# Four layers of cross attention on one core: equal value units and a new order in the third and first steps

## The chip, the cores and the metric

The program runs on one core of a Trainium2 chip. The metric is the time of one execution in device microseconds (us). All data is 32-bit floating point. The profiled execution took 2264.95 us, of which 2263.2 us lie between its first and its last instruction.

## What is computed

64 batches of 128 positions with 160 channels go through four attention layers, one after the other; each layer reads the same context of 77 tokens with 256 channels. 20 heads of 8 channels. Cut to what matters:

```python
q = heads(x @ Wq); k = heads(ctx @ Wk); v = heads(ctx @ Wv)
out = softmax(q @ k.T / sqrt(8)) @ v                   # layers 0 to 2
x = x + merge(out) @ Wo + bo
# layer 3: text = ctx[:, :73], image = ctx[:, 73:]
p = softmax(q @ k_text.T / sqrt(8)); text_out = p @ v_text
sem = normalize(p @ text) @ normalize(image).T         # image scores, per head
fused = q @ k_ip.T / sqrt(8) + 0.5 * sem
ip_out = (softmax(fused) * mask) @ v_ip
x = x + merge(text_out + ip_out) @ Wo + bo
```

The layers in the code are numbered 0 to 3. The norm of `p @ text` is computed through the Gram matrix of the text tokens: `p G p` summed over tokens.

## The kernel before

**Steps.** Each engine runs the same sequence of steps `t`. Step `t` starts item `c = t`: layer `c % 4` of batch `c // 4 - c % 4`. So four steps bring in one new batch, and four batches are under way, each in another layer. The steps are called here by `t % 4`: step 0 starts layer 0 of a batch, step 3 layer 3. An item takes several steps: its scores in step `c`, its second scores (scores transposed, for the exponentials) in step `c + 1`, its product with the values in `c + 2`, its output in `c + 3` (layer 3: `c + 7`, since its image branch comes first). Twenty-four steps are the body of a loop that runs 9 times; the steps before and after it are unrolled.

**The order inside a step** is written by hand for every engine (`step` of each block). TensorE: `scores(t)`, `turn_out`, `queries(t+1)`, `values` (step 3), `product(t-2)`, `project_out`, `image` (the Gram matrix, step 3), `turn_top(t)`, `second(t-1)`, `turn_back(t-2)`. In steps 1 and 2 it also has the four waves of the Gram product, two in each (`gram_wave`); in every even step the keys of one layer for two batches (`keys`: in step 0 at the end, in step 2 ahead of the second scores). One step in 24 has `image_tokens` too.

**PSUM.** `ps_s` (four banks) holds scores, and then the second scores of the item before; `BANKS = (3, 0, 1, 2)` is the order in which they are read. `ps_c` (two buffers) holds products and outputs. `ps_k` is one bank, shared by all units: keys, image tokens, values, Gram matrix and Gram waves. A unit waits until the one before it has been read (`units_done`).

**ScalarE** writes the exponentials (`exps`, from `ps_s` to `p_t`), in layer 3 first in place (`text_exps`), and copies queries, products, outputs, keys and values out of PSUM. **VectorE** reduces the maxima of the scores (`top_of`), subtracts them in layer 3 (`less_top`), multiplies the Gram waves by the probabilities (`weigh`), normalizes the product (`results`, which `turn_out` of the next step waits for through `o_ready`), adds the residual (`new_x`), and computes the image branch in 20 small steps (`image_branch`), each of which waits for the one before. **GpSimd** spreads the keys into blocks (`k_blocks`, two instructions an item), and folds the weighted Gram rows. **SyncE** issues the DMAs, among them the four of each item that carry the maxima to `q_sb` (`move_top`), which the second scores wait for.

**Values.** `values` computes 448 columns (4 layers x 112: two heads of every group of three) and `values_rest` the other 224, after the first have been read; ScalarE copies the first with two instructions of 224 elements and the second with one.

## Time and profile before

| | |
|---|---|
| median of 3 runs | 2264.23 us (2263.96 to 2268.26) |
| the profiled execution | 2264.95 us, span 2263.2 us |
| TensorE matmul busy | 2086.4 us (92%), 26394 matmuls |
| VectorE busy | 1481.7 us (65%) |
| ScalarE busy | 1075.1 us (48%) |
| GpSimd busy | 458.7 us (20%) |
| mean granted TensorE clock | 0.970 |

Lines of the trace give the start in us from the span's start, the time taken, engine, source line, operation, `output<-input` with shapes, and the number of instructions merged in the line. In brackets stands the idle time of that engine ahead of it and what ended it. PE is TensorE's matmul, PEld its weight load, DVE VectorE, ACT ScalarE, POOL GpSimd. An f32 matmul appears as two instructions. The ends of matmuls are modelled, so that a busy TensorE may in truth be waiting; starts are better evidence.

### The profile page before, as it was taken

The page shows a single profiled execution, that of the slowest core. Times are in us where ns is not written, and L with a number is a line of the kernel's source. Part 1 is how long each engine was busy: PE and PEld are TensorE (multiplying, and loading weights), DVE is VectorE, ACT ScalarE, POOL GpSimd, SP SyncE. Part 2 cuts the span into 40 slices and gives each one's busy share as a digit, 9 for nine tenths or more (in the row PEclk, how much of TensorE's full clock was granted, in tenths as well). Part 3 has the DMA queues.
Part 4 walks back from the last instruction along what each step waited for, and adds up shares of the span by engine and source line. Part 5 has one row for each costly group of instructions (what it writes and reads, how often), then busy time and mean ns, then how long its engine had stood idle before and what let it go on. Part 6 is the DMA issues. An engine that isn't in the chain of part 4 may idle for free.

```text
span 2263.2 us, 75842 instructions
## 1 busy us (share of the span) xinstructions
PE 2086.4 (92%) x26394; PEld 1697.5 (75%) x26394; DVE 1481.7 (65%) x4449; ACT 1075.1 (48%) x2733; POOL 458.7 (20%) x870
## 2 busy tenths in 40 slices
PE   2699999999999999999999999999999999999975
PEld 1567877887787788778778877887887788778764
DVE  3236776777677676767767766776676677667654
ACT  0245554455445455544545554554554455555431
POOL 0112122212212221221222122122212222222110
PEclk9889999999999999999999999999999999999975
DMA  3111111211111121112111111211211121111000
GB/s 82 49 43 50 52 43 42 52 50 39 47 52 44 41 52 51 38 46 52 45 41 52 52 38 47 53 44 40 52 52 38 47 53 44 39 53 38 22 10 5
DMA packets 108576, 101.31 MB, mean 45 GB/s; under 512 B 42240, under 2 KB 84952, under 8 KB 108184
## 3 DMA queue, kind: packets, MB, share of 16 engines
q1 hardware_dynamic: 104556, 92.88, 15.1%
q8 instruction: 231, 3.78, 0.7%
q10 hardware_dynamic: 3628, 3.33, 0.6%
q14 instruction: 161, 1.32, 0.2%
HBM read 34.13 MB, written 5.41 MB: 17 GB/s over the span
## 4 chain that ended last, share of the span: by engine, by line
PE 78%; SPq 8%; DVE 5%; issue 4%; DMA 2%; ACT 2%; ACTq 1%; DVEq 0%; POOLq 0%; POOL 0%
PE ps_s L738 11%; PE ps_c L816 10%; PE ps_s L771 8%; PE ps_c L886 6%; PE ps_k L839 6%; PE ps_k L644 5%; PE ps_q L717 5%; PE ps_c L875 4%; PE ps_k L670 4%; PE ps_s L788 4%; PE ps_k L844 4%; SPq L584 3%; PE ps_c L891 3%; PE ps_c L852 2%; SPq L577 2%
## 5 line engine op out<-in xcount | busy, mean ns | idle before, releaser
L1131 DVE TENSOR_REDUCE top<-ps_s 128x6 f32<-128x462 f32 (+3 forms) x1024 | 511.3, 546 | 88.2 <-PE ps_s L738 84.3
L1027 ACT ACTIVATE p_t<-ps_s 116x512 f32<-116x512 f32 (+1 forms) x768 | 372.9, 545 | 48.9 <-PE ps_s L771 46.9
L738 PE MATMUL ps_s<-k_blocks,q_sb 32*128 32x231 f32 (+1 forms) x3584 | 347.8, 384 | 20.3 <-issue 18.5
L816 PE MATMUL ps_c<-p_t,v_rows 116*27 116x128 f32 (+1 forms) x7168 | 288.7, 284 | 14.8 <-DMA v_rows<-v_img 12.3
L738 PEld LDWEIGHTS ps_s<-k_blocks,q_sb 32*128 32x128 f32 x3584 | 229.9, 185 | 84.9 <-issue 31.3
L816 PEld LDWEIGHTS ps_c<-p_t,v_rows 116*27 116x27 f32 (+1 forms) x7168 | 214.1, 108 | 86.5 <-issue 49.3
L1055 ACT ACTIVATE o_t<-ps_c 128x256 f32<-128x256 f32 x256 | 98.1, 383 | 368.3 <-PE ps_c L875 302.7
L1354 POOL TENSOR_TENSOR k_blocks<-k_sb,mask_k 128x231 f32<-128x231 f32 x384 | 211.8, 573 | 267.6 <-PE ps_s L771 252.5
L771 PE MATMUL ps_s<-q_sb,k_blocks 32*116 32x128 f32 (+1 forms) x5376 | 223.8, 283 | 27.7 <-DMA q_sb<-top_t 15.0
L839 PE MATMUL ps_k<-gram,p_t 116*128 116x154 f32 x896 | 210.6, 317 | 41.6 <-DVE weighted L1171 41.6
L771 PEld LDWEIGHTS ps_s<-q_sb,k_blocks 32*116 32x116 f32 (+1 forms) x5376 | 186.3, 175 | 63.7 <-issue 52.0
L1363 POOL TENSOR_TENSOR weighted<-weighted 128x720 f32<-128x720 f32 x64 | 93.0, 1453 | 679.3 <-DVE weighted L1171 679.3
L1171 DVE TENSOR_TENSOR weighted<-ps_k,probs 128x462 f32<-128x462 f32 (+1 forms) x256 | 142.6, 557 | 118.2 <-PE ps_k L844 118.2
L644 PE MATMUL ps_k<-context,wk 128*128 128x154 f32 (+1 forms) x1024 | 159.4, 299 | 40.8 <-DVE minus L1122 40.2
L886 PE MATMUL ps_c<-o_t,wo_lead 128*128 128x128 f32 x1024 | 185.8, 305 | 2.4 <-ACT o_t L1055 2.4
L839 PEld LDWEIGHTS ps_k<-gram,p_t 116*128 116x128 f32 x896 | 137.2, 193 | 66.4 <-DVE weighted L1171 57.9
L886 PEld LDWEIGHTS ps_c<-o_t,wo_lead 128*128 128x128 f32 x1024 | 136.7, 194 | 56.1 <-issue 52.1
L1282 DVE SCALAR_TENSOR_TENSOR x_out<-ps_c,bias,x_work 128x128 f32<-128x128 f32 x64 | 22.5, 351 | 234.9 <-PE ps_c L891 234.9
L644 PEld LDWEIGHTS ps_k<-context,wk 128*128 128x128 f32 x1024 | 142.5, 194 | 42.9 <-issue 42.9
L1040 ACT ACTIVATE u_sb<-ps_c 128x256 f32<-128x256 f32 x256 | 98.1, 383 | 160.9 <-PE ps_c L816 160.9
L844 PE MATMUL ps_k<-gram,p_t 115*128 115x115 f32 (+1 forms) x896 | 166.1, 266 | 0.0
L891 PE MATMUL ps_c<-o_t,wo_tail 32*128 32x128 f32 x1024 | 164.3, 280 | 0.0
(118 smaller groups left out, 3595.3 us busy)
## 6 DMA issues: line engine op xcount, KB each, us to landing
v_rows<-v_img SPq DMA_DIRECT2D x128, 227.4 KB
context<-in_ctx SPq DMA_DIRECT2D x64, 336.0 KB, 3.0
q_sb<-top_t SPq DMA_DIRECT2D x576, 6.0 KB
v_rows<-v_img SPq DMA_DIRECT2D x64, 115.2 KB
v_rows<-v_img SPq DMA_DIRECT2D x64, 112.2 KB
v_rep<-v_dram SPq DMA_DIRECT2D x64, 50.0 KB
q_sb<-top_t SPq DMA_DIRECT2D x192, 2.0 KB
gram<-g_img SPq DMA_DIRECT2D x64, 46.3 KB
```

What stands on the lines that cost most here:

```text
L644: ins = pe.matmul(o[:, :, 0:n], w_rows(wk, l, kt, m, 128), cx_pair(p, kt, 0, n), start=kt == 0, stop=kt == 1)
L738: ins = pe.matmul(ps_s[:, z * 512 + j * GT:z * 512 + j * GT + n], q_sb[c % 3][lo:lo + QUAD, j * S:(j + 1) * S], k_blocks[c % 3][lo:lo + QU ...
L771: ins = pe.matmul(ps_s[0:n, to:to + S], k_blocks[c % 3][lo:lo + QUAD, col:col + n], q_sb[c % 3][lo:lo + QUAD, j * S:(j + 1) * S], start=Tr ...
L816: ins = pe.matmul(ps_c[t % 2][32 * (g % 4):32 * (g % 4) + UC, g // 4 * S:(g // 4 + 1) * S], v_rows[b % NC][0:n, v:v + UC], p_t[c % 3][0:n, ...
L839: pe.matmul(ps_k[:, to:to + 2 * T], p_t[c % 3][0:n, at:at + S], gram[b % NX][0:n, 0:2 * T], start=j == 0, stop=False, skip_group_check=True)
L844: ins = pe.matmul(ps_k[:, to:to + m], p_t[c % 3][0:n, at:at + S], gram[b % NX][0:n, 2 * T:2 * T + m], start=False, stop=True, skip_group_c ...
L886: pe.matmul(ps_c[(t - LAG) % 2][:, j * S:(j + 1) * S], o_rows(wo_lead, l, j), o_t[:, 0:S], start=j == 0, stop=False, skip_group_check=True)
L891: ins = pe.matmul(ps_c[(t - LAG) % 2][:, j * S:(j + 1) * S], o_rows(wo_tail, l, j)[TAIL:LEAD, :], o_t[TAIL:LEAD, S:2 * S], start=False, st ...
L1027: act.activation(to, source, ACT.Exp, scale=SCALE).then_inc(p_ready, 1)
L1131: dve.tensor_reduce(top[c % 2][:, z * BH:z * BH + m], s.rearrange("p (h t) -> p h t", t=T)[:, :, 0:n], AX.X, ALU.max).then_inc(s_top, 1)
L1171: dve.tensor_tensor(weighted[:, lo * T:hi * T], ps_k[:, 0:(hi - lo) * T], probs[:, lo * T:hi * T], ALU.mult).then_inc(w_ready, 1)
L1354: pool.tensor_tensor(k_blocks[c % 3][:, j * GT:(j + 1) * GT].rearrange("p (h t) -> p h t", t=T), keys_of(l, b // 2)[:, at:at + T].unsqueez ...
```

## The change

It changes four things. The values are computed in two equal units, layers 0 and 1 and then layers 2 and 3: each has matmuls of 224 and of 112 columns, and three copies of 112 elements on ScalarE. In step 2 one Gram wave now stands ahead of the second scores, one behind them, and the keys are last. On VectorE, steps 8 to 15 of the image branch stand ahead of `results` in step 0, steps 16 to 18 behind it in the same step (before: in step 1), the new x of layer 3 stands behind `results`, and the wave products follow the waves. On ScalarE the image exponential stands ahead of the exponentials, and the last text exponential at the end of step 3. SyncE and GpSimd are untouched.

```diff
             def units_done(k, t):
...
+                if k is None or t % 4 == 2:
+                    pe.wait_ge(k_evac, raised(k, e_keys, t))
             def keys(k, t):
...
                     units_done(k, t - 1)
+                if e_waves(t):
+                    pe.wait_ge(w_ready, raised(k, e_waves, t, per=2))
...
+            def values_unit(b, u):
+                w = wv[:, :].rearrange("p (l k a n) -> p l k a n", l=L, k=2, a=2)[:, 2 * u:2 * u + 2]
+                third = w.rearrange("p l k a (g i d) -> p l k a g i d", g=TRI, i=2)
+                for kt in range(2):
+                    pe.matmul(ps_k[0:T, 0:2 * VN].rearrange("p (l n) -> p l n", l=2), cx(b, kt, 0, T),
+                              w[:, :, 0, kt, :], start=kt == 0, stop=kt == 1)
+                for kt in range(2):
+                    ins = pe.matmul(ps_k[0:T, 2 * VN:VU].rearrange("p (l g d) -> p l g d", l=2, g=TRI),
+                                    cx(b, kt, 0, T), third[:, :, 1, kt, :, 1, :], start=kt == 0, stop=kt == 1)
+                return ins
...  TensorE, step
-                if e_waves(t) and t % 4 == 1:
+                if e_waves(t):
                     gram_wave(k, t, 0)
-                if e_keys(t) and t % 4 == 2:
-                    keys(k, t)
...
                     second(k, t - 1)
                 if e_waves(t) and t % 4 == 2:
-                    gram_wave(k, t, 0)
+                    gram_wave(k, t, 1)
                 if exists(t - 2):
                     turn_back(k, t - 2)
-                if e_waves(t):
+                if e_waves(t) and t % 4 == 1:
                     gram_wave(k, t, 1)
-                if e_keys(t) and t % 4 == 0:
+                if e_keys(t):
                     keys(k, t)
...  ScalarE
+            def values_out(u):
+                for i in range(GH):
+                    to = v_img[i][:, 2 * u * VL:2 * (u + 1) * VL].rearrange("p (g u) -> p g u", u=UC)
+                    if i < 2:
+                        source = ps_k[0:T, 0:2 * VN].rearrange("p (g u) -> p g u", u=2 * D)[:, :, i * D:(i + 1) * D]
+                    else:
+                        source = ps_k[0:T, 2 * VN:VU].rearrange("p (g u) -> p g u", u=D)
+                    ins = act.activation(to[:, :, i * D:(i + 1) * D], source, ACT.Copy)
+                return ins
...  ScalarE, step
                 if ip(t):
-                    for i in range(4):
+                    for i in range(3):
                         text_exps(k, t, i)
-                for i in range(2):
-                    if exists(t - 1):
-                        exps(k, t - 1, i)
                 if ip(t - 6):
                     image_exp(k, t - 6)
-                for i in range(2, 4):
-                    if exists(t - 1):
+                if exists(t - 1):
+                    for i in range(4):
                         exps(k, t - 1, i)
-                if e_keys(t) and t % 4 == 0:
+                if e_keys(t):
                     keys(k, t)
                 if e_values(t):
                     values_rest(k, t)
+                if ip(t):
+                    text_exps(k, t, 3)
...  VectorE, step
-                if e_waves(t) and t % 4 == 1:
+                if e_waves(t):
                     weigh(k, t, 0)
                 if ip(t - 5):
                     norms(k, t - 5)
                     image_branch(k, t - 5, 1, 8)
-                if ip(t - 6):
-                    image_branch(k, t - 6, 16, 19)
-                if out(t):
+                if out(t) and not ip(out_step(t)):
                     new_x(k, t)
-                if e_waves(t) and t % 4 == 2:
-                    weigh(k, t, 0)
+                if ip(t - 5):
+                    image_branch(k, t - 5, 8, 16)
                 if ip(t - 6):
                     image_branch(k, t - 6, 19, 21)
                     image_weights(k, t - 6)
+                if e_waves(t) and t % 4 == 2:
+                    weigh(k, t, 1)
                 if exists(t - 2):
                     results(k, t - 2)
-                if e_waves(t):
+                if out(t) and ip(out_step(t)):
+                    new_x(k, t)
+                if ip(t - 5):
+                    image_branch(k, t - 5, 16, 19)
+                if e_waves(t) and t % 4 == 1:
                     weigh(k, t, 1)
-                if ip(t - 5):
-                    image_branch(k, t - 5, 8, 16)
```

## Rows read from the trace of the kernel before

**Rows 1.** Who waited for whom on TensorE, 600 to 1800 us: total, times, longest

```profile
PE ps_k L839 <- DVE weighted L1171: 21.4, 36, 0.6
PE ps_s L771 <- DMA q_sb<-top_t: 6.0, 9, 1.1
```

**Rows 2.** Timeline, step 3: last subtraction of the maxima, then second scores

```profile
947.00 0.60 DVE L1146 TENSOR_TENSOR probs<-ps_s,top 128x438 f32<-128x438 f32 x1
...
947.75 0.81 PE L771 MATMUL ps_s<-q_sb,k_blocks 32*116 32x128 f32 x19
```

**Rows 3.** Timeline, end of step 3: exponentials, second value unit, scores of layer 0

```profile
948.82 1.83 ACT L1027 ACTIVATE p_t<-ps_s 116x256 f32<-116x256 f32 x4
...
949.11 0.92 PE L681 MATMUL ps_k<-wv,context 128*77 128x224 f32 x4
...
949.96 1.42 PE L738 MATMUL ps_s<-k_blocks,q_sb 32*128 32x231 f32 x12
...
950.52 0.38 ACT L997 ACTIVATE v_img<-ps_k 77x224 f32<-77x224 f32 x1
950.71 0.31 PEld L738 LDWEIGHTS ps_s<-k_blocks,q_sb 32*128 32x128 f32 x8 [0.19 <-ACT p_t L1027]
```

**Rows 4.** Timeline, step 0 and the start of step 1, VectorE and TensorE

```profile
951.50 1.96 DVE L1131 TENSOR_REDUCE top<-ps_s 128x2 f32<-128x154 f32 x4 [0.20 <-PE ps_s L738]
951.68 0.44 PE L875 MATMUL ps_c<-ident,o_sb 128*128 128x128 f32 x2
...
956.13 0.36 DVE L1284 SCALAR_TENSOR_TENSOR x_work<-ps_c,bias,x_work 32x128 f32<-32x128 f32 x1
...
956.54 1.05 PEld L644 LDWEIGHTS ps_k<-context,wk 128*128 128x128 f32 x8
...
956.85 0.30 DVE L1184 RECIPROCAL recip<-ps_c 128x21 f32<-128x21 f32 x1 [0.36 <-PE ps_c L852]
...
957.18 0.33 DVE L1192 TENSOR_TENSOR o_sb<-ps_c,recip 128x168 f32<-128x168 f32 x1
...
957.73 0.67 PE L738 MATMUL ps_s<-k_blocks,q_sb 32*128 32x231 f32 x8
...
958.73 0.44 PE L875 MATMUL ps_c<-ident,o_sb 128*128 128x128 f32 x2
...
959.27 0.24 DVE L1245 TENSOR_TENSOR z_c<-z_b,rs_y 128x80 f32<-128x80 f32 x1
```

**Rows 5.** The same stretch: GpSimd's key blocks beside image steps 8 and 9

```profile
956.95 1.10 POOL L1354 TENSOR_TENSOR k_blocks<-k_sb,mask_k 128x231 f32<-128x231 f32 x2
...
957.43 0.17 DVE L1234 SCALAR_TENSOR_TENSOR rs_t<-rs_x,rs_y 128x24 f32<-128x24 f32 x1
957.63 0.46 DVE L1237 TENSOR_TENSOR rs_u<-rs_t,rs_y 128x24 f32<-128x24 f32 x1
```

**Rows 6.** Timeline, ScalarE's exponentials in steps 1 and 2, and layer 2's scores

```profile
963.03 0.98 ACT L1027 ACTIVATE p_t<-ps_s 116x256 f32<-116x256 f32 x2 [0.33 <-PE ps_s L771]
...
964.07 1.08 ACT L1027 ACTIVATE p_t<-ps_s 116x512 f32<-116x512 f32 x2
...
965.20 0.31 PEld L738 LDWEIGHTS ps_s<-k_blocks,q_sb 32*128 32x128 f32 x8 [0.20 <-ACT p_t L1027]
...
971.26 1.96 ACT L1027 ACTIVATE p_t<-ps_s 116x256 f32<-116x256 f32 x4
```

**Rows 7.** Timeline, TensorE from step 2's second scores to step 3's scores

```profile
970.49 0.81 PE L771 MATMUL ps_s<-q_sb,k_blocks 32*116 32x128 f32 x19
...
971.58 0.53 PE L839 MATMUL ps_k<-gram,p_t 116*128 116x154 f32 x2
...
973.63 0.53 PE L839 MATMUL ps_k<-gram,p_t 116*128 116x154 f32 x2 [0.61 <-DVE weighted L1171]
...
974.24 0.67 PE L738 MATMUL ps_s<-k_blocks,q_sb 32*128 32x231 f32 x8
```

**Rows 8.** Timeline of another batch, step 0: first matmuls of the image tokens

```profile
721.39 1.07 PE L654 MATMUL ps_k<-ip_six,wkip 128*128 128x24 f32 x8
```

More of the change, by code:

```diff
@@ L47 @@
 VL = TRI * UC
+VU = 2 * (VN + TRI * D)
 LEAD = 128
@@ L625, in units_done @@
                     pe.wait_ge(w_ready, raised(k, e_waves, t, per=2))
+                if k is None or t % 4 == 2:
+                    pe.wait_ge(k_evac, raised(k, e_keys, t))
                 if k is None:
                     pe.wait_ge(six_evac, raised(k, e_six, t))
-                    pe.wait_ge(k_evac, raised(k, e_keys, t))
             def keys(k, t):
@@ L661, in image_tokens @@
                 ins.then_inc(six_psum, 1)
+            def values_unit(b, u):
[8 more added lines that the diff above has]
+                return ins
             def values(k, t):
-                b = values_batch(t)
                 units_done(k, t - 1)
-                w = wv[:, :].rearrange("p (l k a n) -> p l k a n", l=L, k=2, a=2)
-                for kt in range(2):
-                    ins = pe.matmul(ps_k[0:T, 0:L * VN].rearrange("p (l n) -> p l n", l=L), cx(b, kt, 0, T),
-                                    w[:, :, 0, kt, :], start=kt == 0, stop=kt == 1)
-                ins.then_inc(v_psum, 1)
+                values_unit(values_batch(t), 0).then_inc(v_psum, 1)
             def values_rest(k, t):
-                b = values_batch(t)
                 pe.wait_ge(va_evac, raised(k, e_values, t))
-                w = wv[:, :].rearrange("p (l k a g i d) -> p l k a g i d", l=L, k=2, a=2, g=TRI, i=2)
-                for kt in range(2):
-                    ins = pe.matmul(ps_k[0:T, 0:L * TRI * D].rearrange("p (l g d) -> p l g d", l=L, g=TRI),
-                                    cx(b, kt, 0, T), w[:, :, 1, kt, :, 1, :], start=kt == 0, stop=kt == 1)
-                ins.then_inc(vb_psum, 1)
+                values_unit(values_batch(t), 1).then_inc(vb_psum, 1)
             def image(k, t):
@@ L691, in image @@
                     units_done(k, t - 1)
-                at = L * TRI * D
+                at = VU
                 for kt in range(2):
@@ L828, in gram_wave @@
                     pe.wait_ge(p_ready, raised(k, exists, c, per=4))
-                    if e_keys(t):
-                        pe.wait_ge(k_evac, raised(k, e_keys, t))
-                    else:
-                        units_done(k, t - 1)
+                    units_done(k, t - 1)
                 else:
@@ L986, in values @@
                     act.wait_ge(v_ready[(b - 1) % NC], loads(k, b - 1, NC, per=4))
-                for i in range(2):
-                    ins = act.activation(v_img[i][:, :].rearrange("p (g u) -> p g u", u=UC)[:, :, i * D:(i + 1) * D],
-                                         ps_k[0:T, 0:L * VN].rearrange("p (g u) -> p g u", u=2 * D)
-                                         [:, :, i * D:(i + 1) * D], ACT.Copy)
-                ins.then_inc(va_evac, 1)
+                values_out(0).then_inc(va_evac, 1)
+            def values_out(u):
[7 more added lines that the diff above has]
+                return ins
             def values_rest(k, t):
@@ L996, in values_rest @@
                     act.wait_ge(g_psum, raised(k, e_gram, t))
-                act.activation(v_img[2][:, :].rearrange("p (g u) -> p g u", u=UC)[:, :, 2 * D:3 * D],
-                               ps_k[0:T, 0:L * TRI * D].rearrange("p (g u) -> p g u", u=D), ACT.Copy)\
-                   .then_inc(vb_evac, 1)
+                values_out(1).then_inc(vb_evac, 1)
             def queries(k, c):
@@ L1067, in step @@
                     products(k, t - 2)
-                if e_keys(t) and t % 4 == 2:
-                    keys(k, t)
                 if e_six(t):
@@ L1074, in step @@
                 if ip(t):
-                    for i in range(4):
+                    for i in range(3):
                         text_exps(k, t, i)
-                for i in range(2):
-                    if exists(t - 1):
-                        exps(k, t - 1, i)
                 if ip(t - 6):
                     image_exp(k, t - 6)
-                for i in range(2, 4):
-                    if exists(t - 1):
+                if exists(t - 1):
+                    for i in range(4):
                         exps(k, t - 1, i)
-                if e_keys(t) and t % 4 == 0:
+                if e_keys(t):
                     keys(k, t)
@@ L1157, in image @@
                     dve.wait_ge(g_ready[(b - 1) % NX], loads(k, b - 1, NX, per=4))
-                at = L * TRI * D
+                at = VU
                 dve.tensor_tensor(g_img[:, T:2 * T], ps_k[0:T, at:at + T], mask_g[:, :], ALU.mult)
```

## The prediction

> **What bounds the kernel now.** I read the waits first, then the timeline of one ordinary batch, 942 to 974 us, step by step and engine by engine. TensorE shows few waits: in the 1200 us looked at, 36 waits for the weighting of a Gram wave, 21.4 us together, about one a batch of 0.6 us; and 9 for the DMA of the maxima, 6.0 us [rows 1]. But TensorE's ends are modelled, so the gaps between its starts are what counts. Three more places turn out to be held by other engines.
>
> First, step 3: the second scores start at 947.75, 0.15 us after VectorE's last subtraction ends at 947.60 [rows 2]. TensorE has spare time ahead of that point. Second, scores of layer 0: from their start to `turn_out` they take 951.68 - 949.96 = 1.72 us [rows 3, 4], where those of layer 1 take 958.73 - 957.73 = 1.00 us [rows 4]; the difference is a wait for the last bank of exponentials, which end at 950.65, and the weight loads go on at 950.71 [rows 3]. Third, layer 2's scores do the same: exponentials end at 965.15, weight loads go on at 965.20 [rows 6]. The work repeats every 31.74 us or so; some batches differ, see below.
>
> I take the shift of each point within this batch, in us, plus is later.
>
> **Step 3, values.** The first unit loses 448 - 336 = 112 columns times four instructions. It stands ahead of the second scores, which wait for VectorE anyway [rows 2]: gain 0. The cover is VectorE's chain of maxima; it does not change. The second unit grows. Its four matmuls of 224 columns took 0.92 us with the last one's depth, and the next group starts 949.96 - 949.11 = 0.85 after the first, 0.21 each [rows 3]. Four of 112 columns are added: half of 0.21 each is 0.42, four full ones 0.85 if the weight load and not the columns set the pace, and 0.37 at least. I take 0.42, since the rate follows columns in the nearest row. Scores of layer 0 start at 949.96 + 0.42 = 950.38.
>
> **Step 3, last text exponential.** Without it ScalarE is free when the second scores arrive. In step 2 exponentials start 971.26 - 970.49 = 0.77 after the second scores and last 1.96 [rows 6, 7]. So here 947.75 + 0.77 + 1.96 = 950.48 (before 950.65). The third bank of the scores is wanted 0.1 to 0.2 after their start, at 950.5: the wait is gone, and scores take 1.00 instead of 1.72. `turn_out` comes at 951.38: shift **-0.30**. The moved exponential has the whole of layer 0's scores and `turn_top` ahead of its reader: 0.
>
> **Step 3, value copies.** One copy of 0.38 us at 950.52 becomes three of 112 elements; no row has that size with this pattern. Bounds for the three: 0.38 (fixed cost nil) and 1.14 (three times the old one). I take 0.70, between, from the two old copies of 224, which together took less than two singles. They start when the larger unit is done, about 950.57, and end at 951.27, before 950.90. VectorE's two Gram image instructions wait for this and then its maxima of layer 0 follow: they started at 951.50 after 0.20 us of idleness [rows 4], so they can take 0.17 of the 0.37. Shift of the maxima **+0.20**: 951.70.
>
> **Step 0, the image steps.** This is where I expect the price. VectorE runs without a break from the maxima to the end of `new_x`: 951.50 to 956.49, 4.99 us [rows 4]. Now 951.70 + 4.99 = 956.69. There steps 8 to 15 follow, ahead of `results`. Before they took 957.43 to 959.51, 2.08 us [rows 4, 5], of which 0.46 - 0.17 = 0.29 is one slow instruction, step 9, where step 8, of the same size, takes 0.17 [rows 5]. So 1.8 us clean. `results` then take 957.51 - 956.85 = 0.66 [rows 4]. With 0.1 or so for overlaps off: 956.69 + 1.80 + 0.66 - 0.12 = 959.03, and `turn_out` of step 1 can start at about 959.1. TensorE itself would be there at 958.73 - 0.30 = 958.43. The old order had 1.22 us of slack at this point (957.51 to 958.73); the new one is short by 0.7 us even if nothing disturbs. Queued behind the waiting `turn_out` is everything: queries, product, waves. Shift here, clean: **+0.4**.
>
> Disturbance: the slow instruction, at 957.63, has two inputs in SBUF and lies in GpSimd's second key block (956.95 to 958.05, two of 0.55); it ends 0.04 after that [rows 5]. Step 8 at 957.43, at the end of the first block, went undisturbed. In the new order steps 8 and 9 come 0.8 us earlier, at 956.6 and 956.8, and GpSimd 0.3 earlier, at 956.65: they meet both key blocks instead of one. If each block holds such an instruction up for about 0.4 us of its 0.55 (that fits both rows), step 9 ends 0.27 late and step 10 0.58 late. Bounds: 0 (they slip between) and 0.8 (both held until GpSimd is done at 957.75). I take 0.58. That makes 959.68, and `turn_out` of step 1 shifts by **+0.95**.
>
> The Trainium skill, page "SBUF — State Buffer", section "SBUF: two separate sides", says of this that VectorE with two SBUF inputs and GpSimd share one port pair under an exclusive lock that is held for the whole instruction, and that the loser fully blocks. The slow step 9 agrees; the undisturbed step 8 inside a block does not quite. By the page alone the delay would be the 0.8 of my bound, and the batch 0.2 us slower still.
>
> **Step 1.** `new_x` and the image weights lose three small steps ahead of them and are not late. The image exponential leaves the middle of the exponentials: they lasted 965.15 - 963.03 = 2.12 and will last 1.96 [rows 6], and layer 2's scores wait 0.16 less. **-0.15**.
>
> **Step 2.** A wave of eight weight loads takes the keys' place of eight ahead of the second scores: 0, within 0.1 either way. Second scores to next scores took 974.24 - 970.49 = 3.75 [rows 7], with the 0.61 us wait in it. Now: 1.09 to the wave (971.58 - 970.49), and the short wave with its weighting about 1.09 until the keys may start (the wave 0.7, its product on VectorE 0.3 and a handover; `turn_back` hides in it, and about 0.25 us of wait remains), then the keys, 957.73 - 956.54 = 1.19 to the next scores [rows 4], plus 0.03 for 154 columns: 3.40. **-0.35**. VectorE has `results` and `new_x` of layer 3 done before the next maxima; the keys' copy ends well before `values`. The new wait for that copy costs 0, as three units of other work stand between.
>
> **Sum of an ordinary batch:** +0.95 - 0.15 - 0.35 = **+0.45** us. The shifts of step 0's `turn_out` (-0.30) and of the maxima (+0.20) are inside the +0.95.
>
> **Other batches.** One in six has the image tokens ahead of step 0's `turn_top`, 1.07 us in their first group alone [rows 8]: TensorE is so late there that VectorE is not missed, and that batch gains the rest. Its second scores in step 2 wait for the DMA, whose chain starts at the maxima of step 0, so 0.30 and 0.35: -0.65. One in six has the loop's branch between steps 3 and 0, several us in which ScalarE catches up anyway: there +0.42 - 0.35 = +0.07. Per six batches 4 x 0.45 - 0.65 + 0.07 = +1.22 us. 64 batches less the ramps are some 10.3 such groups: **+12.6 us**. On the profiled 2264.95 that gives 2277.5; its span is 1.75 less, and it lies 0.7 above the median of the runs. I say 2277.
>
> **The rivals.** (a) *The image steps run clean, or nearly:* GpSimd's blocks do not hold them up. Then an ordinary batch has +0.37 - 0.50 = -0.13, six batches -1.1, all -11 us: 2253. It decides where `turn_out` of step 1 is less than about 0.65 late; above, the kernel is slower. For: step 8 went undisturbed. Against: the overlap in time is larger than before [rows 5]. (b) *No give-back:* VectorE is early enough, `turn_out` comes at -0.3. Then -0.30 - 0.15 - 0.35 = -0.8, minus 0.6 per six for the others: -3.8 x 10.3 = -39 us, 2225. Against it speaks the 0.7 us by which the sum misses. DMA of the maxima would take some of it, since it already ends waits in 9 of 36 batches [rows 1]. (c) *A draw:* the delay is the old 0.29 us: 4 x 0.16 - 0.6, nil, 2264. (d) *Worse:* blocked by 0.8 or copies at 1.14 us, or 0.85 for the second unit: +0.7 to +0.9 a batch, +23 to +31 us, 2291. (e) *The equal units bring their 0.4 us in step 3,* because the second scores are not held by VectorE: they start 0.4 earlier, -26 us on top. The distance of 0.15 from the subtraction speaks against it.
>
> **How the numbers follow.** Forecast 2277, 0.40; (d) 0.13; (c) 0.17; (a) 0.21; (b) with (e) 0.09. A measurement of this kernel tells 0.2% (4.5 us) from no change. Slower 0.53, same 0.17, faster 0.30. Range: from 2248 (under case a, leaving b and e out) to 2292.
>
> **What the new profile would show.** `turn_out` of step 1 waiting for `o_sb`, about 1.3 us in four of six batches, with steps 8 to 15 directly ahead of `results`: right. Steps of 0.4 us and more among them: GpSimd. Scores of layer 0 at 1.0 us to `turn_out`. No wait of 0.6 us ahead of a wave, one of 0.25 ahead of step 2's keys. Second scores of step 3 still 0.15 after the subtraction. Wrong would be: `results` early in step 0, or second scores of step 2 waiting for the DMA in every batch.

## The result and the profile after

The changed kernel took 2273.96 us (median of 17 runs, 2267.94 to 2279.71), the kernel before 2266.86 us (17 runs, 2255.66 to 2270.93). The ratio is 1.0033, 95% interval 1.0021 to 1.0045: slower by a third of a per cent. Forecast was 2277. The step was forecast at 12.6 us and measured at 7.1. The profiled execution of after has a span of 2267.2 us against 2263.2. Part 1 of its page:

```profile
PE 2039.8 (90%) x26906; PEld 1725.7 (76%) x26906; DVE 1499.4 (66%) x4449; ACT 1108.6 (49%) x2925; POOL 459.7 (20%) x870
```

TensorE has 512 more matmuls and is less busy than before. It waits more. Who waited for whom on TensorE, 600 to 1800 us of after (total, times, longest); this answers [rows 1]:

```profile
PE ps_c L877 <- DVE o_sb L1193: 33.6, 30, 1.7
PE ps_s L776 <- DVE probs L1147: 13.0, 36, 0.6
PE ps_s L743 <- issue: 11.3, 6, 2.0
PE ps_k L648 <- DVE weighted L1172: 9.2, 36, 0.3
PE ps_s L776 <- DMA q_sb<-top_t: 6.2, 6, 1.2
```

The old wait for the weighting of a wave, 0.6 us once a batch, is gone. What is left of it is 0.3 us ahead of step 2's keys. `turn_out` (L877) now waits for VectorE's `results`, 33.6 / 30 = 1.1 us each time, a wait that did not exist. In the timeline of after, step 0 and the start of step 1 of one batch, TensorE, VectorE and GpSimd, one sees why (answers [rows 4, 5]):

```profile
694.85 1.94 DVE L1132 TENSOR_REDUCE top<-ps_s 128x2 f32<-128x154 f32 x4
...
699.46 0.36 DVE L1285 SCALAR_TENSOR_TENSOR x_work<-ps_c,bias,x_work 32x128 f32<-32x128 f32 x1
699.85 0.18 DVE L1235 SCALAR_TENSOR_TENSOR rs_t<-rs_x,rs_y 128x24 f32<-128x24 f32 x1
...
700.07 0.27 DVE L1238 TENSOR_TENSOR rs_u<-rs_t,rs_y 128x24 f32<-128x24 f32 x1
700.25 1.10 POOL L1357 TENSOR_TENSOR k_blocks<-k_sb,mask_k 128x231 f32<-128x231 f32 x2
700.37 0.49 DVE L1240 SCALAR_TENSOR_TENSOR rs_y<-rs_u,rs_y 128x24 f32<-128x24 f32 x1
700.90 0.50 DVE L1235 SCALAR_TENSOR_TENSOR rs_t<-rs_x,rs_y 128x24 f32<-128x24 f32 x1
701.43 0.18 DVE L1238 TENSOR_TENSOR rs_u<-rs_t,rs_y 128x24 f32<-128x24 f32 x1
...
702.14 0.24 DVE L1246 TENSOR_TENSOR z_c<-z_b,rs_y 128x80 f32<-128x80 f32 x1
702.41 0.29 DVE L1185 RECIPROCAL recip<-ps_c 128x21 f32<-128x21 f32 x1
...
702.74 0.33 DVE L1193 TENSOR_TENSOR o_sb<-ps_c,recip 128x168 f32<-128x168 f32 x1
...
703.13 0.44 PE L877 MATMUL ps_c<-ident,o_sb 128*128 128x128 f32 x2 [1.03 <-DVE o_sb L1193]
```

VectorE runs from 694.85 to 703.07 with no wait listed. Image steps 8 to 15 (699.85 to 702.38) stand ahead of `results` (702.41), and TensorE stands for 1.03 us. Steps of 0.18 us take 0.49 and 0.50 while GpSimd writes its two key blocks (700.25 to 701.35, 0.55 each): both blocks are met, as forecast.

Time can be measured batch by batch with VectorE's copy into `s_ip`, which comes once in each. Two neighbours before, then the same two of after; the start is the first column:

```profile
618.08 0.25 DVE L1143 COPY s_ip<-ps_s 128x96 f32<-128x96 f32 x1
649.81 0.25 DVE L1143 COPY s_ip<-ps_s 128x96 f32<-128x96 f32 x1
```

```profile
625.33 0.25 DVE L1144 COPY s_ip<-ps_s 128x96 f32<-128x96 f32 x1
657.89 0.25 DVE L1144 COPY s_ip<-ps_s 128x96 f32<-128x96 f32 x1
```

31.73 us became 32.56. The whole loop shows six kinds of batch, in this order: three ordinary, one with image tokens, one ordinary, one that crosses the loop's end. Means over eight periods of six batches in the one profiled execution of each kernel, in us:

| kernel | ordinary batches (1, 2, 3, 5) | image tokens | crossing | six batches |
|---|---|---|---|---|
| before | 31.73, 32.26, 31.54, 31.74 | 34.81 | 35.66 | 197.73 |
| after | 32.56, 32.45, 32.18, 32.28 | 34.35 | 35.13 | 198.95 |

So the four ordinary batches lost 2.21 us together, the one with image tokens gained 0.46, the crossing gained 0.53, and a period lost 1.22. Over eight periods that is +9.8 us. The rest of the span (the first and last batches, which are unrolled, and what lies around them) is 5.8 us shorter than before: 675.6 against 681.4.

The end of that rest is TensorE's clock and not less work. After the last copy into `s_ip` the kernel before runs 38.9 us more and after 32.5, 6.4 less. TensorE's clock has two levels, 2.4 GHz (a granted clock of 1.00) and 1.2 GHz (0.50). In each line: a stretch, its length, busy us and instructions of each engine, then the granted clock, the DMA engines' share and GB/s. First the kernel before, whole tail and then from the product to the last Gram wave's weighting; then the same two of after:

```profile
2224.30:2263.20 38.90, 21.87 (x102) 18.08 (x102) 15.55 (x62) 5.14 (x13) 1.76 (x2) 0.50 0.02 5
2229.16:2246.39 17.23, 14.34 (x73) 11.88 (x73) 5.07 (x16) 1.31 (x4) 0.00 (x0) 0.50 0.02 5
```

```profile
2234.70:2267.20 32.50, 15.53 (x102) 12.71 (x102) 15.52 (x62) 5.04 (x13) 1.76 (x2) 0.71 0.02 6
2239.56:2250.47 10.91, 8.00 (x73) 6.52 (x73) 4.42 (x15) 1.20 (x4) 0.00 (x0) 1.00 0.00 0
```

The same 73 matmul instructions took 17.23 us at the lower level and 10.91 at the higher, and that is 6.3 of the 6.4 us.

### The profile page after: what moved, and what is told of

The parts are those of the page before. It is cut to its first block and busy times, and to the rows that moved or that the text cites. A ratio compares the mean times of both kernels' runs of the same rounds, so it can differ in the third digit from the quotient of the medians.

```text
span 2267.2 us, 77136 instructions
## 1 busy us (share of the span) xinstructions
PE 2039.8 (90%) x26906; PEld 1725.7 (76%) x26906; DVE 1499.4 (66%) x4449; ACT 1108.6 (49%) x2925; POOL 459.7 (20%) x870
## 5 line engine op out<-in xcount | busy, mean ns | idle before, releaser
L743 PE MATMUL ps_s<-k_blocks,q_sb 32*128 32x231 f32 (+1 forms) x3584 | 309.2, 377 | 17.2 <-issue 15.6
L821 PE MATMUL ps_c<-p_t,v_rows 116*27 116x128 f32 (+1 forms) x7168 | 283.2, 280 | 15.9 <-DMA v_rows<-v_img 13.4
L743 PEld LDWEIGHTS ps_s<-k_blocks,q_sb 32*128 32x128 f32 x3584 | 210.1, 186 | 59.1 <-issue 33.1
L841 PE MATMUL ps_k<-gram,p_t 116*128 116x154 f32 x896 | 201.3, 306 | 4.7 <-DVE weighted L1172 4.7
L1016 ACT ACTIVATE top_t<-ps_q 20x128 f32<-20x128 f32 x192 | 50.9, 265 | 245.1 <-PE ps_q L807 216.7
L1357 POOL TENSOR_TENSOR k_blocks<-k_last,mask_k 128x231 f32<-128x231 f32 x128 | 70.7, 573 | 385.0 <-PE ps_s L776 385.0
```

Of the source, the lines that this page charges most:

```text
L743: ins = pe.matmul(ps_s[:, z * 512 + j * GT:z * 512 + j * GT + n], q_sb[c % 3][lo:lo + QUAD, j * S:(j + 1) * S], k_blocks[c % 3][lo:lo + QU ...
L821: ins = pe.matmul(ps_c[t % 2][32 * (g % 4):32 * (g % 4) + UC, g // 4 * S:(g // 4 + 1) * S], v_rows[b % NC][0:n, v:v + UC], p_t[c % 3][0:n, ...
L841: pe.matmul(ps_k[:, to:to + 2 * T], p_t[c % 3][0:n, at:at + S], gram[b % NX][0:n, 0:2 * T], start=j == 0, stop=False, skip_group_check=True)
L1357: pool.tensor_tensor(k_blocks[c % 3][:, j * GT:(j + 1) * GT].rearrange("p (h t) -> p h t", t=T), keys_of(l, b // 2)[:, at:at + T].unsqueez ...
```

## The experiments

The theory: the price is VectorE's order in step 0, made worse by GpSimd, and the parts in step 2 and 3 are worth their small gains. The table gathers what all kernels gave: the median time; its ratio to the runs of before that went with it, whose medians lay between 2265.2 and 2266.9 us; and in the one profiled execution the sum of the four ordinary batches and the two others, means in us as above. The last column says in how many of the eight crossings TensorE's clock fell to 1.2 GHz, which the part on the crossing takes up.

| kernel | us | ratio (95%) | ordinary | image tokens | crossing | fell in |
|---|---|---|---|---|---|---|
| before | 2266.86 | 1 | 127.27 | 34.81 | 35.66 | 8 |
| after | 2273.96 | 1.0033 (1.0021 to 1.0045) | 129.48 | 34.35 | 35.13 | 4 |
| after_results_first | 2243.31 | 0.9902 (0.9880 to 0.9923) | 127.07 | 34.29 | 34.83 | 4 |
| before_image_first | 2311.81 | 1.0202 (1.0179 to 1.0225) | 131.68 | 34.79 | 35.61 | 4 |
| after_pool_waits | 2247.64 | 0.9917 (0.9895 to 0.9939) | 127.35 | 34.25 | 34.96 | 5 |
| results_first_pool | 2232.16 | 0.9864 (0.9839 to 0.9888) | 126.22 | 34.35 | 34.39 | 2 |
| no_image_moves | 2238.30 | 0.9875 (0.9849 to 0.9901) | 126.09 | 34.21 | 34.29 | 4 |
| before_waves | 2254.96 | 0.9949 (0.9931 to 0.9967) | 126.01 | 34.47 | 36.05 | 7 |
| before_equal_units | 2251.04 | 0.9949 (0.9927 to 0.9970) | 127.28 | 34.52 | 34.68 | 5 |
| before_text_last | 2248.66 | 0.9933 (0.9908 to 0.9958) | 126.75 | 34.55 | 35.23 | 5 |
| before_units_text | 2253.62 | 0.9943 (0.9920 to 0.9966) | 127.35 | 34.51 | 34.61 | 4 |
| before_padded | 2275.02 | 1.0039 (1.0022 to 1.0057) | 127.20 | 34.84 | 36.99 | 8 |
| results_first_pool_gram | 2211.78 | 0.9765 (0.9738 to 0.9792) | 125.59 | 33.23 | 34.83 | 5 |
| no_image_moves_gram | 2201.23 | 0.9721 (0.9695 to 0.9748) | 125.09 | 33.11 | 33.81 | 2 |

**The order in step 0: after_results_first and before_image_first.** One takes the image steps out of the way of `results` in after, the other puts them there in before and changes nothing else.

```diff
  VectorE, step, after_results_first
-                if ip(t - 5):
-                    image_branch(k, t - 5, 8, 16)
...
                     new_x(k, t)
                 if ip(t - 5):
-                    image_branch(k, t - 5, 16, 19)
+                    image_branch(k, t - 5, 8, 19)
```

> The changed kernel with one move undone: VectorE's results of step 0 stand ahead of image steps 8 to 15 again (16 to 18 follow them). My theory, that the image steps ahead of the results are what the change loses by: turn_out of step 1 no longer waits (30 waits, 33.6 us in 600 to 1800 us of the changed kernel); the next maxima come 0.9 us later than in the kernel before and turn_top of step 1 takes part of the wait over, about 0.5 us. So about 0.5 us less a batch in four of six batches and a little in the others: 2245 to 2255 us, 0.7% faster than the kernel before. Rival, that the value units or the waves cost it: within 0.3% of the changed kernel.

```diff
  VectorE, step, before_image_first
+                if ip(t - 5):
+                    image_branch(k, t - 5, 8, 16)
                 if exists(t - 2):
                     results(k, t - 2)
                 if e_waves(t):
                     weigh(k, t, 1)
-                if ip(t - 5):
-                    image_branch(k, t - 5, 8, 16)
```

> The kernel before with one move made: image steps 8 to 15 ahead of the results in step 0, nothing else. My theory: the results end 1.8 us later plus 0.3 to 0.7 us for GpSimd's key blocks, less the 0.36 us that VectorE idled ahead of them and the 1.22 us of slack: turn_out of step 1 waits 0.6 to 1.0 us in four of six batches, 2265 + 26 to 43 = 2291 to 2308 us, 1.2% to 1.9% slower than before. Rival (the change loses elsewhere): within 0.3% of before.

Measured: 2243.31, and the wait for `o_sb` has left TensorE's list; 2311.81, and it has appeared. TensorE's wait in before_image_first, 600 to 1800 us:

```profile
PE ps_c L875 <- DVE o_sb L1192: 30.5, 27, 1.7
```

The ordinary batches of before_image_first lost 131.68 - 127.27 = 4.4 us, 1.1 each; those of after_results_first won 2.4. So this one order carries a price in either kernel. The batch with image tokens stayed at 34.79 against 34.81 in before_image_first, which is the prediction's claim that TensorE is late there anyway. The time of before_image_first came out 4 us above the band that was expected; after_results_first came out 2 us below its own.

**GpSimd's part: after_pool_waits.** The key blocks of step 1 wait until `results` are done, so that they don't lie beside the image steps.

```diff
  GpSimd, keys of item c
+                if ip(c - 7):
+                    pool.wait_ge(o_ready, raised(k, exists, c - 4))
```

> The changed kernel, with GpSimd's key blocks of step 1 made to wait until the results of step 0 are written, so that they lie beside no image step ahead of them. They are needed only 5 us later. In the changed kernel steps 8 to 15 take 2.53 us, 1.80 without disturbance. If GpSimd holds VectorE up: they take 1.8 to 1.9, turn_out of step 1 comes 0.6 us earlier in four of six batches, 2274 - 27 = 2247 us, 0.8% faster than the kernel before. If the slow steps have another cause: no change from the changed kernel, 2274.

Measured 2247.64. Timeline of after_pool_waits, the same image steps, VectorE and GpSimd:

```profile
693.96 0.18 DVE L1235 SCALAR_TENSOR_TENSOR rs_t<-rs_x,rs_y 128x24 f32<-128x24 f32 x1
...
694.18 0.27 DVE L1238 TENSOR_TENSOR rs_u<-rs_t,rs_y 128x24 f32<-128x24 f32 x1
...
694.48 0.18 DVE L1240 SCALAR_TENSOR_TENSOR rs_y<-rs_u,rs_y 128x24 f32<-128x24 f32 x1
...
696.61 0.44 PE L877 MATMUL ps_c<-ident,o_sb 128*128 128x128 f32 x2 [0.41 <-DVE o_sb L1193]
696.64 1.10 POOL L1359 TENSOR_TENSOR k_blocks<-k_sb,mask_k 128x231 f32<-128x231 f32 x2 [2.23 <-DVE o_sb L1193]
```

The third step, 0.49 us in after, takes 0.18; steps 8 to 15 take 693.96 to 695.86 = 1.90 us, where after has 2.53; TensorE's wait is 0.41 instead of 1.03. The key blocks cost 0.63 us a batch there, and the ordinary batches became 0.53 shorter each (129.48 to 127.35 for four): nearly all of it is on the path. The step of 0.27 is still 0.09 late; in both kernels another GpSimd instruction of 0.32 us, the one that writes `probs`, lies beside it. TensorE's wait for `o_sb` is down to 15.3 us in 27, so the order alone and GpSimd's blocks are about equal halves of that wait.

**Both removed: results_first_pool, no_image_moves.** The first has the later order and keeps the key blocks away from the image steps. The second has the units, the waves and the text exponential of the change, with the image branch and the image exponential where they were before.

```diff
  results_first_pool: the order of after_results_first, and on GpSimd
+                if ip(c - 7):
+                    pool.wait_ge(ip_step, raised(k, ip, c - 8, per=IP_STEPS, more=18))
```

> after_results_first with GpSimd's key blocks of step 1 waiting until image step 18 is done. There turn_top of step 1 still waits for VectorE's maxima (12.1 us in 37 batches, 0.33 each), which come behind image steps 8 to 18; of these 8 to 15 take 2.2 us with the key blocks beside them. If the blocks are what holds them up: the wait of turn_top goes nearly, 0.3 us a batch, 2243 - 19 = 2224 us, 1.8% faster than the kernel before. If not: 2243 us.

```diff
  no_image_moves: VectorE, step of after
+                if ip(t - 6):
+                    image_branch(k, t - 6, 16, 19)
...
-                if ip(t - 5):
-                    image_branch(k, t - 5, 8, 16)
...
-                if ip(t - 5):
-                    image_branch(k, t - 5, 16, 19)
...
+                if ip(t - 5):
+                    image_branch(k, t - 5, 8, 16)
  ScalarE: image_exp back between the second and third of exps
```

> The changed kernel with the whole image branch where it was before: steps 8 to 15 at the end of step 0, 16 to 18 in step 1, the image exponential in the middle of the exponentials. Equal units, waves and last text exponential as changed. My theory: no wait of turn_out, no wait of turn_top of step 1 (0.33 us in after_results_first), and layer 2's scores wait 0.15 us longer: 2243 - 12 = 2231 us, 1.5% faster than before. Rival (moving the fused scores early is worth more than it costs): 2245 us or more.

Measured 2232.16 and 2238.30, 8 and 7 us above what was expected. In results_first_pool the wait of `turn_top` for VectorE's maxima fell to 3.5 us in 5 batches, from 12.1 in 37 in after_results_first, so GpSimd's blocks were most of that wait too. The ratios of after and no_image_moves, 1.0033 and 0.9875, differ by 1.6%: that is the price of the image moves in the change, and without them it is 1.25% faster than before. Both kernels wait up to 0.7 or 0.8 us for the DMA of the maxima in 11 and 13 batches of those looked at, 5.4 and 7.5 us in all; after did so in six, 6.2 us in all with one of 1.2. A batch that is quicker elsewhere can run into this wait.

**The three other parts alone.** First step 2:

```diff
  before_waves: the edits of the change for waves, keys, weigh and new_x; on TensorE
-                if e_waves(t) and t % 4 == 1:
+                if e_waves(t):
                     gram_wave(k, t, 0)
-                if e_keys(t) and t % 4 == 2:
-                    keys(k, t)
```

> The kernel before with only the waves of step 2 moved (one on each side of the second scores, the keys last, with their copies, products and the new x of layer 3 behind the results). My theory: the 0.61 us wait goes and about 0.25 us ahead of the keys comes, 0.35 us less in every batch: 2265 - 22 = 2243 us, 1.0% faster. Rival (the wait goes elsewhere, to the DMA of the maxima or to the keys): within 0.2% of before.

Measured 2254.96. The ordinary batches are 31.44, 31.93, 31.23, 31.41: each about 0.32 shorter, as said. But the crossing became longer, 36.05 on average and up to 37.95 in single ones, and took part of it back. In four of the eight crossings the clock stood at 1.2 GHz for 6.8 us, where in before no stretch was longer than 3.4.

```diff
  before_equal_units: values_unit and values_out of the change, nothing else
```

> The kernel before with the equal value units alone. My theory: nothing. The 0.38 us by which the second unit grows delays the start of layer 0's scores, but these wait for the last exponentials anyway, 0.74 us behind their start; turn_out of step 0 stays at its place: 2265 us, within 0.2%. Rival one, that the columns count: +0.38 us a batch, 2289 us. Rival two, that the smaller first unit brings the second scores forward: 2240 us.

```diff
  before_text_last: ScalarE
-                    for i in range(4):
+                    for i in range(3):
                         text_exps(k, t, i)
...
+                if ip(t):
+                    text_exps(k, t, 3)
```

> The kernel before with the last text exponential at the end of step 3, nothing else. The exponentials of step 3 end 0.16 us earlier (0.77 + 1.96 behind the second scores), and so do the waits of layer 0's scores: 0.16 us in five of six batches, 2265 - 8 = 2257 us, 0.4% faster. Rival, that the whole 0.5 us of the moved exponential is gained: 2238 us.

```diff
  before_units_text: both edits
```

> The kernel before with the equal units and the last text exponential together. Alone, the units left ordinary batches as they were and the exponential gave 0.16 us. Together turn_out of step 0 comes 0.2 us earlier, as in the changed kernel: the units' 0.38 us stay hidden behind the exponentials. Ordinary batches 0.2 us shorter, 2265 - 11 = 2254 us, and besides what the loop's crossing takes, up to 12 us either way. Rival: the 0.38 us show as soon as the wait for the exponentials is shorter, and the two together are 0.2 us a batch slower than the exponential alone.

Measured 2251.04, 2248.66 and 2253.62. With equal units alone the ordinary batches sum to what they were (127.28 against 127.27), which is what was expected, and still the kernel is 0.5% faster: a miss of 14 us. The equal sum hides two shifts. `turn_out` of step 0 came 0.20 us earlier in three of the four kinds, and the batch behind the one with image tokens became 0.25 longer. TensorE's waits in before_equal_units:

```profile
PE ps_k L841 <- DVE weighted L1177: 21.9, 37, 0.6
PE ps_s L773 <- DVE probs L1152: 13.2, 37, 0.6
```

The second line is the time that the smaller first unit saves, 0.36 us a batch, now stood out in front of the second scores, as a wait for the subtraction. In before it was hidden in a TensorE that looked busy. With that the rival of 0.4 us gained in step 3 has fallen. The gain of before_equal_units is instead in the crossing, 34.68 against 35.66 (a period gains 1.24 in all, of which 0.98 there), and in the unrolled ends (672.7 us against 681.4); part of both is TensorE's clock, see the next part. The text exponential gives 0.52 in four ordinary batches, and 0.43 in the crossing.

The two together (before_units_text) gave the time that was expected, but not where it was expected. Its ordinary batches sum to 127.35, 0.08 more than in before and 0.60 more than with the exponential alone, where 0.2 less in each was expected; this is what the rival in the expectation said. In three of the four kinds `turn_out` of step 0 stood 4.85 us behind the copy into `s_ip` in before, 4.67 with the exponential moved, 4.65 with equal units and 4.65 with both. Either edit removes the same wait, so the gains don't add.

**The crossing: before_padded, and TensorE's clock.** Four waits that have long been fulfilled go into TensorE's step 3, ahead of `turn_back`. They change no order and no work.

```diff
+                if t % 4 == 3:
+                    pe.wait_ge(setup, 1)
...
```

> The kernel before with four waits in each step 3 of TensorE that are long fulfilled, so that only the place of its instructions changes. Ordinary batches stay at 31.5 to 32.2 us. If the batch that crosses the loop's end depends on how the instructions lie (it took 35.7 us in the kernel before and 34.3 with the equal units alone, whose ordinary batches were the same), it moves here too, by up to 1.5 us, and the time by up to 12 us either way; if it is the work that counts, the time is 2265 us and no batch changes by 0.3 us.

Measured 2275.02, ratio 1.0039 (1.0022 to 1.0057). The ordinary batches are those of before (127.20 against 127.27); the crossing is 36.99 against 35.66. TensorE's wait at the loop's end in before, then in before_padded, 600 to 1800 us:

```profile
PE ps_s L738 <- issue: 14.3, 6, 2.5
```

```profile
PE ps_s L738 <- issue: 20.3, 6, 3.7
```

Six crossings, one us more in each. Four waits that hold nothing up move the time of this kernel by 0.4%, as much as the change under study, most of it where the loop's branch is. The profiled execution of before_padded is the slowest of its twelve, 6 us above the median, so its trace shows the difference larger than the medians do. No run here tells which property of the code sets the length of the pause.

The traces show a second cause that the padding doesn't need. Behind the pause TensorE's clock falls to 1.2 GHz in some crossings, for 3.4 us and sometimes 6.8. Three stretches of before_text_last: a crossing, the stretch inside it at the lower level, and a crossing of the same execution without one:

```profile
1169.42:1204.91 35.49, 32.67 (x414) 26.67 (x411) 22.95 (x69) 16.67 (x42) 7.02 (x13) 0.95 0.16 45
1176.40:1179.60 3.20, 3.20 (x35) 2.42 (x35) 3.05 (x8) 0.98 (x3) 0.00 (x0) 0.50 0.01 3
1366.31:1400.06 33.75, 31.04 (x414) 25.49 (x411) 22.57 (x70) 16.67 (x42) 7.01 (x13) 1.00 0.17 47
```

In that kernel the five crossings with a fall took 35.93 us on average and the three without 34.05; in before_equal_units 35.16 and 33.87, in no_image_moves 35.04 and 33.54. All eight crossings of before have a fall, and none took under 35.2 us. Its 35.66 is 0.98 above the mean of before_equal_units, but only 0.50 above the mean of those five that have a fall too. In before_padded all eight have one, three of them of 6.8 us; the five others took 36.58 on average. By these numbers the longer pause is most of its 1.33 us and the longer falls are the rest.

The clock also goes with the time of whole executions. Of 54 executions of the kernel before that ran beside the experiments, the 19 with a mean granted clock of 0.967 or less took 2268.6 us on average, the 16 with 0.971 or more 2260.1. Why the clock falls in one crossing and not in the next, and how the code bears on it, is not shown. The crossing column holds one execution of each kernel, so differences of some tenths in it, and in the unrolled ends, are weak evidence.

**What is late next: results_first_pool_gram and no_image_moves_gram.** SyncE issues DMAs one behind the other. SyncE's queue in no_image_moves, start and time from the first issue to the last in each line:

```profile
789.63 2.21 SPq L585 DMA_DIRECT2D q_sb<-top_t  x3
791.89 3.21 SPq L568 DMA_DIRECT2D v_rows<-v_img  x4
795.23 0.78 SPq L578 DMA_DIRECT2D gram<-g_img  x1
796.05 1.58 SPq L578 DMA_DIRECT2D gram<-w_img  x1
797.67 1.51 SPq L578 DMA_DIRECT2D gram<-g_img  x2
799.30 0.82 SPq L585 DMA_DIRECT2D q_sb<-top_t  x1
```

The maxima of the next item stand behind four values and four Gram DMAs. In both new kernels the Gram DMAs go one step later:

```diff
  SyncE, step, behind move_top
-                if e_gram(t - 1):
-                    place_gram(k, t - 1)
+                if e_gram(t - 2):
+                    place_gram(k, t - 2)
```

> results_first_pool, and the four DMAs of the Gram matrix issued one step later, behind the four of step 1's maxima instead of ahead of them (they are wanted two batches later). In results_first_pool the second scores of step 2 wait for the DMA of the maxima 5.4 us in 37 batches, 0.7 us in every sixth. If SyncE's queue of 16 issues is what is late: these waits go, 0.15 us a batch, 2232 - 9 = 2223 us, 1.8% faster than the kernel before. If the DMAs' own time is: no change, 2232.

> no_image_moves with the same move of the Gram DMAs. Its second scores wait 7.5 us in 37 batches for the DMA of the maxima: 2238 - 13 = 2225 us, 1.7% faster than before, equal with results_first_pool_gram. Then moving the fused image scores is worth nothing once the queue is out of the way.

Measured 2211.78 and 2201.23, 11 and 24 us below what was expected, and not equal as expected: with the image branch as before the kernel is 0.5% faster, 0.50 us of it in four ordinary batches. SyncE's queue in no_image_moves_gram:

```profile
613.83 3.09 SPq L585 DMA_DIRECT2D q_sb<-top_t  x4
616.96 3.29 SPq L568 DMA_DIRECT2D v_rows<-v_img  x4
621.18 3.11 SPq L585 DMA_DIRECT2D q_sb<-top_t  x4
624.41 0.84 SPq L578 DMA_DIRECT2D gram<-g_img  x1
```

TensorE's waits there, 600 to 1800 us, all of them:

```profile
PE ps_s L776 <- DVE probs L1150: 13.4, 38, 0.6
PE ps_s L743 <- issue: 11.8, 6, 2.4
PE ps_k L648 <- DVE weighted L1175: 9.7, 38, 0.3
```

No wait for a DMA is left between 600 and 1800 us. The batch with image tokens went from 34.21 to 33.11, the ordinary ones from 126.09 to 125.09. no_image_moves_gram is the best version of the study: 2.8% faster than before, and it beats both kernels. It is the changed kernel with its units, waves and last text exponential, the image branch as before, and the Gram DMAs later.

## Why the prediction was right

The forecast (2277, slower) and its main mechanism held: VectorE's order in step 0 costs more than the other parts give. The time was 3 us lower, but the kernel before was also 2.6 us above the three runs on which the sum stood, so 12.6 us were forecast and 7.1 measured. By its own steps, shifts in us from VectorE's copy into `s_ip`, means over the 32 ordinary batches of the eight periods unless a run is named:

| step | forecast | measured |
|---|---|---|
| second scores of step 3 | 0 | -0.01 |
| layer 0's scores | +0.42 | +0.38 |
| `turn_out` of step 0 | -0.30 | -0.15 |
| VectorE's maxima of layer 0 | +0.20 | -0.06 |
| image steps held up by GpSimd | 0.58 | 0.73 (one batch) |
| `turn_out` of step 1 | +0.95 | +1.05 |
| image exponential, and wave in the keys' place | -0.15 | -0.22 |
| rest of step 2 | -0.35 | -0.28 (before_waves: -0.32 a batch) |
| ordinary batch | +0.45 | +0.55 |
| batch with image tokens | -0.65 | -0.46 |
| crossing | +0.07 | -0.53 |
| six batches | +1.22 | +1.22 |

**Right, and shown by a run of its own.** The give-back on VectorE (before_image_first, after_results_first), GpSimd beside the image steps (after_pool_waits), step 2 (before_waves), and the first value unit hidden under the subtraction (before_equal_units). The shift of `turn_out` in step 1 is +0.90 in batches of the kind that the prediction read, against +0.95. But the four kinds differ: +1.34, +0.86, +1.10, +0.90. In the first behind the crossing VectorE's maxima of layer 0 begin 4.98 us after the copy and not 4.5 to 4.6, so its `results` are later still; one batch was not the pattern of all.

Timeline of after, step 3, last subtraction, second scores and the value copies (answers [rows 2, 3]):

```profile
690.50 0.60 DVE L1147 TENSOR_TENSOR probs<-ps_s,top 128x438 f32<-128x438 f32 x1
691.25 0.81 PE L776 MATMUL ps_s<-q_sb,k_blocks 32*116 32x128 f32 x19 [0.62 <-DVE probs L1147]
...
692.61 0.92 PE L673 MATMUL ps_k<-wv,context 128*77 128x224 f32 x4
693.37 0.55 PE L676 MATMUL ps_k<-wv,context 128*77 128x112 f32 x4
693.85 0.86 PE L743 MATMUL ps_s<-k_blocks,q_sb 32*128 32x231 f32 x10
693.95 0.57 ACT L996 ACTIVATE v_img<-ps_k 77x112 f32<-77x112 f32 x3
```

The subtraction ends at 691.10 and the second scores start 0.15 later, as in [rows 2]; what was hidden is now written as a wait of 0.62. From 692.61 to 693.85 the second unit takes 1.24 us, 0.39 more than the 0.85 of [rows 3]: columns set the pace, not the number of weight loads.

**Terms that were mis-sized.** The three value copies took 0.57 us, where 0.70 stood in the sum between bounds of 0.38 and 1.14, and they began 0.13 sooner after the copy into `s_ip` than it said. So VectorE's maxima came 0.06 early and not 0.20 late, about 0.26 to the good. GpSimd cost 0.73 instead of 0.58, of which 0.63 are the key blocks (after_pool_waits). These cancel in part, so the sum's accuracy at this point was partly luck. The shift of `turn_out` in step 0 was put down to the moved text exponential; before_equal_units has it without that move. The rival of clean image steps (2253) has nearly been built: after_pool_waits took 2247.64.

**The step that failed** is the crossing, put at +0.42 - 0.35 = +0.07. It gained 0.53. The +0.42 of the larger second unit did not arrive: the first scores behind the branch begin 5.5 us after the copy in both kernels, and TensorE's pause at the branch is shorter by about as much (14.3 us in six before, 11.3 after). `turn_out` of step 1 came 0.35 later, for which the sum had nothing, and the steps behind it gave back more than the 0.35 of the sum. The clock has a small share: of after's eight crossings the four with a fall took 35.28 us, the four without 34.98. The prediction had no term for the branch's pause or the clock behind it, with which a crossing moved between 33.8 and 37.0 us from kernel to kernel (table above). The batch with image tokens gained 0.46 instead of 0.65, and the ordinary ones lost 2.21 instead of 4 x 0.45 = 1.80. The errors are +0.41, +0.19 and -0.60: that the period came to +1.22 exactly is because they cancel, and that is luck.

**Also not in the sum:** it took 10.3 periods, as if first and last batches behaved like the others. The eight periods of the loop gave +9.8 us and the rest gave -5.8. Of that rest the tail behind the last copy is -6.4, and it is TensorE's clock, as shown above. From the last copy to the tail's second reduction into `q_n` it took 23.65 us in before and before_waves, all of it at 1.2 GHz; 21.6 to 21.7 in six kernels with 14 to 15 us at that level, among them before_image_first and before_equal_units, whose image orders differ; 18.95 with 8.7 us at it in two; and 17.3 with 4.2 us at it in after and two others. Whether the changed order is what lets the clock rise there is not shown: all the kernels with the image exponential moved have a tail of 34.2 us or less, all the others 36.8 or more. At the other end after spent 54.6 us at the lower level before its first copy into `s_ip`, the kernel before 27.3, and reached that copy 4.3 us later; how much of this the clock costs is not separated. So the +7.1 of the medians is a difference of orders with some us of clock on both sides.

## What to carry to other kernels

An instruction that is taken from the end of an engine's step and put ahead of a result that others wait for costs its whole length, plus what its new neighbours on other engines do to it, less the slack at that result; read the slack at that result first (here 1.22 us, against 1.9 to 2.5 us of work moved ahead of it), and read it in every kind of batch. When a change brings a small gain, look at what the quicker part now meets: here it was the queue in which one engine issues DMAs, and moving four of them gave 1.0% and 1.6%, more than the change itself moved. Between builds of a kernel with a hardware loop, compare batches inside the loop and not only total times, since four waits without effect moved the total by 0.4%. And read the granted clock of each stretch before its time is put down to the code: a tail that seemed 6.4 us shorter had the same work at another clock.

## What the runs showed of the hardware

A crossing of the loop's end can take a us more for code that holds nothing up: TensorE's longest wait there rose from 2.5 to 3.7 us with four fulfilled waits in each step 3, and the median rose by 8 us.

Behind such a pause TensorE's granted clock fell from 1.00 to 0.50 (2.4 to 1.2 GHz), for 3.4 or 6.8 us, in 2 to 8 of eight crossings of a kernel. A batch with a fall of 3.4 us took 1.3 to 1.9 us more than one without in the same execution (before_equal_units, no_image_moves, before_text_last), 0.3 in after and 0.7 in before_image_first, where TensorE waits for VectorE in the same batch. In the tail 73 matmul instructions with their waits took 17.23 us at 0.50 and 10.91 at 1.00.

VectorE and GpSimd hold each other up only in part. In after, the image steps that began inside a key block, at 700.37 and 700.90, ended 0.06 and 0.05 us after the block did, if its two halves are 0.55 us each (ends on GpSimd are rough); they took 0.49 and 0.50 us instead of 0.18. In the kernel before, an equal step that began 0.07 us ahead of the end of a block took 0.17 and was not held [rows 5]. The Trainium skill, page "SBUF — State Buffer", section "SBUF: two separate sides", says that whichever starts first holds the shared port pair for its whole instruction and the other fully blocks. A step that stood for the whole block and then took its own 0.18 us would end 0.18 after it, and the step in [rows 5] would have been 0.07 late; neither is seen, though 0.07 us is little beside such ends. The two blocks added 0.63 us of their 1.10.

An issue of the DMAs that carry maxima, values or Gram rows takes SyncE's queue about 0.8 to 1.0 us (four in 3.1 to 3.9 in the lines above), so eight of them ahead of a wanted one are more than 6 us.
